# TensorE's order in the two weighted sums: the two units of a step together, and the fp32 product in eights

## What is computed

```
# second network
a   = exp(e - e_max[dst]) / denom[dst]
out = segment_sum(a[:, None] * nfeat[src], dst)
# fourth network
messages = x[src] * edge_weights[:, None]
out = segment_sum(messages, tgt)
```

## Time and profile before

| what | value |
|---|---|
| median of three runs | 4672.75 us |
| the profiled execution's own time | 4673.2 us |
| its span | 4671.4 us |
| mean granted TensorE clock | 0.897 |
| PE busy | 3843.2 us (82%), 103291 instructions |
| PEld busy | 3137.0 us (67%) |
| DVE busy | 3633.4 us (78%) |
| ACT busy | 1937.0 us (41%) |
| POOL busy | 946.3 us (20%) |
| chain that ended last, by line | L1123 19%, L1096 15%, L1163 13%, L930 10%, L1084 3% |
| L1123 (fp32 product) PE | 1020.4 us busy, 7252 records, 392 ns each |
| L1096 (weights) PE | 961.8 us busy, 56832 matmuls, 184 ns each |
| L784 (copy of weights) ACT | 964.2 us busy, 1184 copies, 814 ns each |
| L779 (copy of counts) ACT | 288.8 us busy, 592 copies, 488 ns each |

### The profile page before, as it was taken

The page is one execution under the profiler, slowest core; times in us unless marked ns, Lnnn a source line. Parts: engine busy times, 40 slices in busy tenths (PEclk is TensorE's granted clock), DMA queues, the critical chain, the costliest instruction groups (busy, mean ns, idle before and its releaser), DMA issues.

```text
span 4671.4 us, 227804 instructions
## 1 busy us (share of the span) xinstructions
PE 3843.2 (82%) x103291; PEld 3137.0 (67%) x103291; DVE 3633.4 (78%) x4577; ACT 1937.0 (41%) x2437; POOL 946.3 (20%) x810
## 2 busy tenths in 40 slices
PE   5631875949629499999999997998998899999996
PEld 4631774948629467777777776997997566666665
DVE  5974686787875899889889986555555999999996
ACT  5200102001010066666666664664664454554543
POOL 0565667653244151000000000000000000000000
PEclk8975695968858799999999998998998899999998
DMA  6743252633415311111111113553553000000000
GB/s 156 261 140 49 74 168 73 185 109 96 132 22 154 105 57 57 62 57 57 62 57 57 63 54 118 177 176 126 178 178 103 8 11 10 11 10 10 11 10 18
DMA packets 240228, 404.31 MB, mean 87 GB/s; under 512 B 110258, under 2 KB 167860, under 8 KB 239524
## 3 DMA queue, kind: packets, MB, share of 16 engines
q1 hardware_dynamic: 213928, 383.16, 26.5%
q0 software_dynamic: 25472, 10.79, 1.2%
q10 hardware_dynamic: 184, 0.08, 0.0%
HBM read 287.89 MB, written 110.03 MB: 85 GB/s over the span
## 4 chain that ended last, share of the span: by engine, by line
PE 68%; DVE 13%; issue 6%; POOL 4%; DMA 2%; ACT 2%; DVEq 0%; SPq 0%; ACTq 0%
PE psum L1123 19%; PE psum L1096 15%; PE psum L1163 13%; PE psum L930 10%; PE psum L1084 3%; DVE space L1653 2%; POOL gath L628 2%; POOL heads_d L620 2%; PE psum L898 1%; PE psum L886 1%; PE psum L872 1%; PE psum L1172 1%; DVE space L1433 1%; DVE V L1418 1%; PE psum L1007 1%
## 5 line engine op out<-in xcount | busy, mean ns | idle before, releaser
L784 ACT COPY space<-psum 128x784 f32<-128x784 f32 x1184 | 964.2, 814 | 674.8 <-PE psum L1096 673.4
L1096 PEld LDWEIGHTS psum<-space 64*128 64x128 bf16 x56832 | 828.1, 94 | 317.5 <-issue 161.7
L1096 PE MATMUL psum<-space 64*128 64x49 bf16 x56832 | 961.8, 184 | 91.2 <-issue 46.2
L1123 PE MATMUL psum<-space,X 128*64 128x256 f32 x7252 | 1020.4, 392 | 2.5 <-ACT space L784 1.8
L1653 DVE TENSOR_TENSOR space<-space 128x2352 bf16<-128x2352 bf16 x592 | 813.8, 1375 | 0.0
L930 PE MATMUL psum<-table,space 128*128 128x56 bf16 x24300 | 677.3, 189 | 112.2 <-DVE space L1303 76.2
L930 PEld LDWEIGHTS psum<-table,space 128*128 128x128 fp8e4 x24300 | 664.0, 96 | 125.4 <-issue 118.1
L1645 DVE TENSOR_TENSOR space<-space,V 128x2048 bf16<-128x2048 bf16 x592 | 720.2, 1217 | 0.0
L1163 PE MATMUL psum<-space 128*128 128x192 bf16 x7252 | 629.3, 247 | 11.8 <-ACT space L817 11.8
L1300 DVE TENSOR_REDUCE space<-psum 128x1512 f32 (+1 forms) x300 | 518.6, 1731 | 134.7 <-PE psum L930 132.1
L1163 PEld LDWEIGHTS psum<-space 128*128 128x128 bf16 x7252 | 595.7, 98 | 37.6 <-issue 36.8
(11 more groups left out here) (286 smaller groups left out, 2894.3 us busy)
## 6 DMA issues: line engine op xcount, KB each, us to landing
space<-adj_d SPq DMA_DIRECT2D x148, 784.0 KB, 4.3
space<-onehots SPq DMA_DIRECT2D x240, 432.0 KB
adj_d<-space SPq DMA_DIRECT2D x222, 192.0 KB
onehots<-space SPq DMA_DIRECT2D x60, 432.0 KB, 3.2
space<-digit_rows SPq DMA_DIRECT2D x60, 378.0 KB
adj_d<-space SPq DMA_DIRECT2D x74, 208.0 KB
space<-cw_d SPq DMA_DIRECT2D x37, 160.0 KB, 2.3
cw_d<-space SPq DMA_DIRECT2D x4, 1184.0 KB, 13.2
```

Source lines behind the costliest of these rows:

```text
L784: nc.scalar.copy(A[:, h, :, b * P:(b + 1) * P].rearrange("p a (w s) -> p w a s", w=2)[:, :, :, c:c + UC], psum[:, 2 + 2 * (k % 2):4 + 2 * ...
L1096: mm = nc.tensor.matmul(psum[:, 2 + 2 * (k % 2) + w, c * NB:(c + 1) * NB], ohlo[lo:hi, ring, col // 2, :, col % 2], ohw[lo:hi, ring, r, co ...
L1123: mm = nc.tensor.matmul(pb[6][half:half + F, 0:2 * P], X[:, a, :], A[:, 1 - h, a, :], start=(a < 2), stop=(a >= NB - 2))
```

## The change

TensorE's program alone changes, and the constant PART from 4 to 8, which makes EVERY 2 and leaves MIXED at 13. The function for a unit becomes one for a step: both units' counts, then both units' weights. It is called at even k. The fp32 product then comes at odd k up to 11, eight sub-blocks at a time, and its last sub-block at k = 12 as before. The semaphores and their values are the same; `codes_ready` and `hot_ready` are waited for once in a step as before, `adj_made` and `wgt_made` before each unit's run, as before. Placing stays at k = 2 and transposing at k = 14, each now behind both units of its step.

```diff
--- before.py
+++ after.py
@@ -63,7 +63,7 @@
 GU = KC // UC
 HC = 2 * UC
 HS = P // HC
-PART = 4
+PART = 8
 EVERY = PART // 4
 STORES = [(0, 13), (13, 25), (25, 37), (37, NB)]
 MIXED = (NB - 1) // PART * EVERY + 1
@@ -1068,41 +1068,41 @@
             for n in range(1, 4):
                 carries(2 * LAYERS + n, back=int(n == 2))
 
-            def products_of_unit(n, i, h, k):
-
-                u = i * (4 * GU) + (n * NDB * 2 * GU + h * 2 * GU + k + 1)
-                hot = i * (2 * HS) + (n * NDB * HS + h * HS + k // 2 + 1)
-                early = k if isinstance(i, int) and n + i + h == 0 else 2
-                ring = (k // 2) % 2
+            def products_of_step(n, i, h, t):
+
+                hot = i * (2 * HS) + (n * NDB * HS + h * HS + t + 1)
+                units = [i * (4 * GU) + (n * NDB * 2 * GU + h * 2 * GU + 2 * t + e + 1) for e in range(2)]
+                first = isinstance(i, int) and n + i + h + t == 0
+                ring = t % 2
                 if n == 0:
-                    if k % 2 == 0:
-                        pe.wait_ge(codes_ready, hot)
-                    if early >= 2:
-                        pe.wait_ge(adj_made, u - 2)
+                    pe.wait_ge(codes_ready, hot)
+                    for e in range(2):
+                        if not first:
+                            pe.wait_ge(adj_made, units[e] - 2)
+                        for c in range(UC):
+                            col = e * UC + c
+                            mm = nc.tensor.matmul(psum[:, e, c * NB:(c + 1) * NB], ohlo[:, ring, col // 2, :, col % 2],
+                                                  hi_both[:, ring, col // 2, :, col % 2], start=True, stop=True)
+                        mm.then_inc(adj_psum, 1)
+                pe.wait_ge(hot_ready, hot)
+                for e in range(2):
+                    if not first:
+                        pe.wait_ge(wgt_made, units[e] - 2)
                     for c in range(UC):
-                        col = (k % 2) * UC + c
-                        mm = nc.tensor.matmul(psum[:, k % 2, c * NB:(c + 1) * NB], ohlo[:, ring, col // 2, :, col % 2],
-                                              hi_both[:, ring, col // 2, :, col % 2], start=True, stop=True)
-                    mm.then_inc(adj_psum, 1)
-                if k % 2 == 0:
-                    pe.wait_ge(hot_ready, hot)
-                if early >= 2:
-                    pe.wait_ge(wgt_made, u - 2)
-                for c in range(UC):
-                    col = (k % 2) * UC + c
-                    for r in range(3):
-                        for w in range(2):
-                            lo, hi = KC * w, KC * w + KC
-                            mm = nc.tensor.matmul(psum[:, 2 + 2 * (k % 2) + w, c * NB:(c + 1) * NB], ohlo[lo:hi, ring, col // 2, :, col % 2],
-                                                  ohw[lo:hi, ring, r, col // 2, :, col % 2], start=(r == 0), stop=(r == 2))
-                mm.then_inc(wgt_psum, 1)
+                        col = e * UC + c
+                        for r in range(3):
+                            for w in range(2):
+                                lo, hi = KC * w, KC * w + KC
+                                mm = nc.tensor.matmul(psum[:, 2 + 2 * e + w, c * NB:(c + 1) * NB], ohlo[lo:hi, ring, col // 2, :, col % 2],
+                                                      ohw[lo:hi, ring, r, col // 2, :, col % 2], start=(r == 0), stop=(r == 2))
+                    mm.then_inc(wgt_psum, 1)
 
             def pair(n, i, h, unit=True, mix=True, put=True):
 
                 D = i * 2 + (n * NDB + h)
                 for k in range(2 * GU):
-                    if unit:
-                        products_of_unit(n, i, h, k)
+                    if unit and k % 2 == 0:
+                        products_of_step(n, i, h, k // 2)
                     if put and k == 2:
                         pe.wait_ge(slots_copied, D - 1)
                         pe.wait_ge(spot_ready, D - 1)
```

## The result

The changed kernel takes **4656.38 us** (median of 6 runs, 4646.98 to 4662.32) against 4673.24 us for the kernel before in the same session (6 runs): ratio 0.996, 95% interval 0.9946 to 0.9973. It is 0.4% faster. The forecast was 4515 us, 3.4% faster, with a range from 4485 to 4610. The sign is right; of the 158 us only 17 came, and the time lies outside the range.

What follows compares the result with a forecast made beforehand. TensorE was taken to bound both sums, VectorE close behind; pairs falling from 31.63 to 29.1 and 26.56 to 24.7 us save 36 x (2.53 + 1.86) = 158 us from 4672.75: 4515 us, range 4485 to 4610.

Steps and rivals of the forecast that it cites:

- Part 1: Six full steps a pair: two units together change kind once instead of twice, saving 2.0 us (first sum), 1.4 us (second).
- Part 3: Wait on `adj_made` or `wgt_made` inside a doubled run: taken as 0, at most 1.8 and 0.9 us a pair.
- Part 4: L1131's wait (0.32 us a pair) goes, VectorE's idle time largely too; 0.2 us a pair allowed for `adj_made`.
- the second form of the supply rival: ScalarE's PSUM copies late, TensorE waiting on `adj_made` or `wgt_made` every step, 0.25 us each; both forms together 0.2.
- Part 5: Same number of matmuls, copies, DMAs and gathers; placing (L1111) a unit later costs nothing, else a fraction of a us a pair.
- VectorE's floor: VectorE's own work in a pair, which nothing shortens: 28.5 us in the first sum, 24.3 us in the second.
- Supply in the long runs: Instruction supply halts TensorE 0.25 us in each full step's long runs, 1.5 us a pair: 4615 us; both forms together 0.2.
- the sum: Savings and waits added along TensorE's way through a pair, set beside VectorE's work: 29.1 and 24.7 us a pair.
- The sign that was named beforehand: Forecast wrong through supply if L1096's "issue" or ScalarE waits grow by 1 us a pair.
- no change: VectorE is the true limit already and TensorE's busy time is stretch: within 9 us of 4673; chance 0.04.
- The clock rival: TensorE's pauses in steps 7 and 0 lower its clock, 2.3 us more a full step, 4846 us with two; chance 0.06.

Runs made afterwards that it cites:

- experiment 7: Changed kernel with two 98-column weights matmuls in place of three of 49, third part left out, sums not the reference's: 4550.64 us.
- experiment 10: Kernel before with two 98-column weights matmuls in place of three of 49, output not the sum of the three parts: 4729.68 us.
- experiment 2: Changed kernel with seven product sub-blocks at each odd k up to 13, and placing (L1111) moved to k = 1: 4681.37 us.
- experiment 4: Changed kernel without the third bf16 part of the weights, 32 instead of 48 matmuls a unit: 4475.16 us in one run.
- experiment 12: Changed kernel with the middle weights matmul issued as 25 and 24 columns in each step's second unit, same result: 4902.99 us.
- experiment 9: Kernel before with 96 no-operations a pair that never reached the program, so a repeat of that kernel: 4676.75 us.
- experiment 8: Changed kernel with 96 no-operations a pair that never reached the program, so a repeat of that kernel: 4651.59 us.
- experiment 11: Changed kernel with two 98-column weights matmuls in place of three of 49 in each step's second unit alone, sums wrong there: 4522.7 us.

## Why the prediction was wrong, step by step

- **Part 1, the price of a change of kind: right, a little low.** Full steps are 3.78 and 3.22 us for 3.8 and 3.25; two units of the old order, twice 2.07 and twice 1.74 us, are 0.36 and 0.26 us longer, where 0.33 and 0.23 were forecast. With supply out of the way the change of order saves 2.67 and 2.23 us a pair (experiments 7 and 10) for 2.53 and 1.86. On the Trainium skill's rule (TensorEngine Tiling, Key Properties) that a change of tiling mode drains the engine, the runs agree.
- **Part 3, the seam in a doubled run: right at 0.** 16 counts need 0.54 us from their start to the weights (2156.69 to 2157.23), 96 weights 1.36: the old spacings, doubled. The prediction says that no row shows such a seam at full clock, but its own have two runs of 96 weights with one in it, busy 1.74 and 1.65 us. The changed kernel's run is busy 1.42, so what these held was no seam.
- **Part 4, waits.** The wait of L1131 for ScalarE is gone, and ScalarE makes TensorE wait 2.1 us in 1100, so the second form of the supply rival, a late ScalarE, did not come. L1644's wait fell from 104.2 to 54.4 us, less than forecast. TensorE was late for a new reason.
- **Part 5, placing at no cost: right in the time, not in the reason.** VectorE does wait for L1111 now, 38.1 us in the second sum, and for L1139, 29.4 us in the first. They seem to take the place of its earlier ones for L1096: experiment 2 took the first away, the wait for L1096 grew instead, and nothing was gained.
- **VectorE's floor: right.** 28.36 and 24.60 us measured in experiment 4 for 28.5 and 24.3.
- **The step that failed** is in the rival "Supply in the long runs": "the average rate hardly rises, and the eight sub-blocks behind give time to catch up". On it rests the sum, which has no term for instructions. No row set the average rate against a limit. A pair of the first sum needs 7.9 packets and one of the second 6.9 (mean pairs of the changed kernel, 31.40 and 26.59 us, times 251 / 1000 and 156 / 600). At the 3.94 and 3.75 us that experiment 12 shows as the best, that is an estimate of 31.1 and 25.9 us a pair for any of these orders, on average. The kernel before stood at means of 31.68 and 26.67, some 0.6 and 0.8 us above: of 4.4 us to be saved in two pairs, about 1.4 was to be had, and 0.4 came (0.7 between experiments 9 and 8). The row was there: q8, 249 packets in 1000 us. What it meant could not be read from the kernel before alone, but the 8.6 us of "issue" stops in the earlier trace rows were the sign to ask.
- Why eight sub-blocks give no time to catch up can be counted, though the reserve itself is in no trace. A full step of the first sum issues 16 counts, 96 weights and 16 product records, each with its weight load: 256 instructions, one packet, in 3.78 us. Before, the same step took about 4.1 us. The supply is a packet in 3.94 us. So before, full steps were slower than supply and a reserve could build up for the steps without product; after, they are a little faster than supply, and nothing builds up. Steps 6, 7 and 0 then follow each other with almost no product between them, 224 instructions in 1.9 us each. The first of them still gets through (4 stops in 1100 us), the other two mostly do not (59 of the 95 stops).
- **The price of this rival** was set at 0.25 us a step, 4615 us. It is 2.3 and 1.9 us a pair, the mean pairs of 31.40 and 26.59 less the forecast of 29.1 and 24.7; TensorE's "issue" stops are 2.2 and 1.6 us of it. The sign that was named beforehand, L1096's "issue" growing by 1 us a pair, is the one that came. Its own sum also has a slip: 24.7 and 1.5 are 26.2, not 26.0, which makes it 4623 us. The chance of 0.2 and the range both followed from the same error: the rival's worst case was never worked out, and that would have put "no change" inside the range.
- **The clock rival: the clock did fall, its price was not paid.** The granted clock fell to 0.99 and 0.98 in the stretches that had 1.00. At 1% and 2% of 1037 and 856 us of TensorE's busy time that is 10 and 17 us at most, an estimate; it did not decide the sign. That the stops bring it about was not tested apart. With TensorE busy 1000.64 of 1020 us the clock was 1.00 (experiment 7). It can fall with either kind of idleness: to 0.97 in the first sum of experiment 12, which waits for instructions, and to 0.93 in the second sum of experiment 4, which waits for VectorE. The two stretches of experiment 4, both with waits almost only for VectorE:

```profile
1700.00:2700.00 1000.00, 889.41 (x26034) 670.41 (x26025) 973.10 (x1422) 677.17 (x1183) 186.04 (x86) 1.00 0.19 64
3700.00:4400.00 700.00, 617.42 (x17498) 444.42 (x17489) 683.75 (x792) 358.46 (x510) 0.00 (x0) 0.93 0.04 10
```

What stays open: what sets the rate of a packet in 3.75 to 4.0 us. A packet is in transfer for 1.05 us (median) of these, and all of them fill 1.8% of the DMA engines, so it is not their bandwidth. The trace after holds a hint: when TensorE goes on after a stop, the next packet's transfer starts 1.3 us later (median), it takes 1.05, and TensorE goes on 1.4 after its end, 3.8 us in all. That looks like a packet that is asked for only when TensorE has come to the one before; no run tried it. No version was found that keeps all three parts and beats both kernels clearly: experiments 4, 7 and 11 leave some out. A 98-column matmul that adds two parts into the same 49 columns of PSUM would cut instructions without that flaw, if it can be done; it was not tried.

## What to carry to other kernels

When an engine's program is written out in full, set the instruction queue's packets beside the time: the instructions of a repeated stretch over 256, times the time for a packet, was here an estimate of what no reordering got below on average. "Issue" stops in the middle of a run of like matmuls, even a few microseconds of them, are the sign to ask; look whether they end a fixed time after a packet of that queue. If they do, cut instructions (fewer, wider matmuls) before cutting time. To price a reordering, run it once with the suspected ceiling lifted, in both versions: here the same change is worth 17 us under the ceiling and 179 us without it.

## What the runs showed that was not expected

- Over 1000 us of the first sum and 600 us of the second, TensorE's instructions arrived at no more than one packet of 256 in 3.94 us and 3.75 us, 15 ns an instruction, in any run.
- Each of the 98 stops of the changed kernel's first sum ended 1.2 to 1.6 us after such a packet had landed.
- More columns in fewer instructions were faster: a third more weights columns took 106 us off the changed kernel.
- A semaphore increment of its own on TensorE's queue behind a run of matmuls cost 48 to 89 ns, in the open, sixteen of them 0.8 to 1.4 us.
- Two stretches with TensorE busy 89% and 88% and the same kind of wait, for VectorE, were granted 1.00 and 0.93 of the clock (experiment 4). The waits of L1096 for VectorE were up to 0.7 us in the first and up to 1.3 us in the second; which difference decides was not tried.
